# Row maxima on two 64-row tiles of TensorE, one head of a pair in each

## The reference

```
h = layernorm(x) * (1 + ca) + sa
q = h Wq^T; latent = h Wkv_down^T; k = latent Wk_up^T; v = latent Wv_up^T     # 8 heads of 64
attn = softmax(q k^T / 8) ; x = x + ga * (attn v) Wo^T
h = layernorm(x) * (1 + cb) + sb
x = x + gb * (h W^T + pooled(h) disha)
```

## Time and profile before

| | |
|---|---|
| time, median of 3 runs | 3648.74 us (3648.51 to 3649.03) |
| the profiled execution | 3651.17 us, span 3649.2 us |
| granted TensorE clock | 0.983 of full speed |
| TensorE busy | 97% |
| VectorE / ScalarE / GpSimd busy | 67% / 46% / 69% |
| DMA | 9.9% of 16 engines |

### The profile page before, as it was taken

One profiled execution on the slowest core, in us unless ns is written; L12 is line 12 of the kernel. 1 busy time (PEld: TensorE's weight loads), 2 busy tenths in 40 slices (PEclk: granted clock), 3 DMA queues, 4 the chain that ended last, 5 costly groups with the idle time before them and its releaser, 6 DMA issues.

```text
span 3649.2 us, 50991 instructions
## 1 busy us (share of the span) xinstructions
PE 3530.1 (97%) x15014; PEld 1840.0 (50%) x15014; DVE 2446.3 (67%) x2846; ACT 1684.6 (46%) x3075; POOL 2515.4 (69%) x1513
## 2 busy tenths in 40 slices
PE   5999999999999999999999999999999999999997
PEld 3444555545454554545545455454555545555454
DVE  4667667676676767657676576766767667676663
ACT  1445445444454545445454354543545445454443
POOL 1677767676776767668677676866767677686775
PEclk7999999999999999999999999999999999999998
DMA  1101010010101001010010100101010010100101
GB/s 55 35 20 48 24 56 21 30 48 27 47 26 55 18 27 53 24 51 18 33 47 24 51 27 27 50 27 48 21 41 36 27 48 27 53 18 33 35 30 32
DMA packets 98076, 129.24 MB, mean 35 GB/s; under 512 B 11120, under 2 KB 62448, under 8 KB 97776
## 3 DMA queue, kind: packets, MB, share of 16 engines
q1 hardware_dynamic: 97776, 125.64, 9.9%
HBM read 41.11 MB, written 16.81 MB: 16 GB/s over the span
## 4 chain that ended last, share of the span: by engine, by line
PE 94%; DVE 3%; issue 2%; ACT 1%; POOL 0%; DMA 0%; SPq 0%; DVEq 0%; POOLq 0%; ACTq 0%
PE ps_mix L543 28%; PE ps_max L593 18%; PE ps_score L564 14%; PE ps_score L566 13%; PE ps_side_b L531 7%; PE ps_side_b L651 5%; PE ps_side_a L638 4%; PE ps_side_b L669 3%; PE ps_side_a L631 1%; PE ps_side_a L658 1%; DVE h_lo L972 1%; PE ps_side_a L608 0%; DVE recip L931 0%; DVE neg_max L950 0%; PE ps_side_a L622 0%
## 5 line engine op out<-in xcount | busy, mean ns | idle before, releaser
L811 POOL TENSOR_TENSOR prob_sum<-prob_sum,probs 128x1024 f32<-128x1024 f32 x768 | 1837.5, 2393 | 575.7 <-ACT probs L710 518.7
L950 DVE TENSOR_REDUCE neg_max<-ps_max 128x1 f32<-128x1024 f32 x1016 | 1243.5, 1224 | 721.1 <-PE ps_max L593 710.9
L710 ACT ACTIVATE probs<-ps_score 128x512 f32<-128x512 f32 x2048 | 1113.0, 596 | 1140.9 <-PE ps_score L566 1129.2
L543 PE MATMUL ps_mix<-probs,values 128*64 128x512 f32 x4096 | 1109.5, 620 | 0.0
L564 PE MATMUL ps_score<-query,key_hi 128*128 128x512 f32 x2048 | 839.8, 410 | 37.2 <-issue 35.8
L566 PE MATMUL ps_score<-query_m,key_lo 128*128 128x512 f32 x2048 | 810.2, 396 | 0.0
L593 PE MATMUL ps_max<-key_hi,query 128*128 128x512 f32 x2032 | 749.8, 450 | 5.1 <-DVE neg_max L950 5.0
L593 PEld LDWEIGHTS ps_max<-key_hi,query 128*128 128x128 f32 x2032 | 304.5, 189 | 830.4 <-issue 433.6
L811 POOL TENSOR_TENSOR prob_sum<-probs 128x1024 f32<-128x1024 f32 x128 | 305.5, 2387 | 457.7 <-ACT probs L710 457.7
L931 DVE RECIPROCAL recip<-recip 128x128 f32<-128x128 f32 x512 | 481.4, 942 | 17.8 <-ACT recip L761 17.8
L564 PEld LDWEIGHTS ps_score<-query,key_hi 128*128 128x128 f32 x2048 | 387.5, 189 | 155.2 <-issue 73.9
(11 more groups left out here) (115 smaller groups left out, 2701.8 us busy)
## 6 DMA issues: line engine op xcount, KB each, us to landing
query_m<-query SPq DMA_DIRECT2D x128, 512.0 KB, 3.2
x_in<-in_L_attn_x_dram SPq DMA_DIRECT2D x16, 1024.0 KB, 5.5
x_mid<-in_L_attn_x_dram SPq DMA_DIRECT2D x64, 256.0 KB, 6.9
out_dram<-x_mid SPq DMA_DIRECT2D x64, 256.0 KB, 2.2
h_t<-gates_scratch SPq DMA_DIRECT2D x16, 256.0 KB, 6.7
query_m<-max_row SPq DMA_DIRECT2D x128, 4.0 KB
mixed<-in_L_wmod_dram SPq DMA_DIRECT2D x1, 1536.0 KB, 11.3
mixed<-in_L_attn_Wq_dram SPq DMA_DIRECT2D x1, 512.0 KB, 4.9
```

The costliest lines, as they stand in the source:

```text
L543: last = nc.tensor.matmul(ps_mix[g % 2][j * R:j * R + R, :], values[par][:, k, :], probs[:, s % RING, j * HALF:(j + 1) * HALF], start=(k = ...
L710: nc.scalar.activation(probs[:, s % RING, half * HALF:(half + 1) * HALF], ps_score[half], ACT.Exp, scale=SCALE).then_inc(exps_done, 1)
L811: nc.gpsimd.tensor_tensor(out=total[:, :], in0=before, in1=probs[:, s % RING, :], op=ALU.add).then_inc(adds_done, 1)
L950: nc.vector.tensor_reduce(neg_max[:, m:m + 1], z.max_bank(m, ps_max, ps_scores)[:, :], AX_X, ALU.max, negate=True).then_inc(maxima_done, 1)
```

## The change

The row-maximum pass is cut otherwise. Before, a step took 128 queries of one head, high and low parts (128 partitions), by 1024 keys. After, a step takes 128 queries of both heads of a pair, with their high parts alone (64 partitions each), by 512 keys: the even head's matmul reads partitions 0 to 63 and writes the first bank, the odd head's reads 64 to 127 and writes the second. The number of steps, of matmuls and of their columns stays the same. For that odd heads keep their high parts on partitions 64 to 127 and their low parts on 0 to 63 of `query`. The scores' second product pairs `query_m` with `key_lo` and its last row must still be a low-part partition, so the copy to `query_m` swaps the halves of the odd head: three DMAs in place of one, and the waits on `query_m_copied` count 48 instead of 16. VectorE's reduction gives two maxima (one per head) of half the keys, into `neg_half`; at the last step of a group a small operation takes the minimum of the two halves (they are negated) into `neg_max`, behind a wait for the reduction, and a new semaphore, `maxima_joined`, tells TensorE's max_row.

```diff
--- before.py
+++ after.py
@@ -272,6 +272,7 @@
         values = [sb(f"values{i}", [P, NT, R]) for i in range(2)]
         query = sb("query", [P, H, T], F32R)
         query_m = sb("query_m", [P, 2, T], F32R)
+        neg_half = sb("neg_half", [P, 2, STEPS])
         neg_max = sb("neg_max", [P, STEPS])
         max_row = [sb(f"max_row{i}", [NT, P], F32R) for i in range(2)]
         probs = sb("probs", [P, RING, T])
@@ -358,6 +359,7 @@
         exps_done = sem("exps_done")
         max_scores_ready = sem("max_scores_ready")
         maxima_done = sem("maxima_done")
+        maxima_joined = sem("maxima_joined")
         full = [sem("a_full"), sem("b_full")]
         a_full, b_full = full
         a_drained = sem("a_drained")
@@ -455,11 +457,14 @@
                             elif j in (2, 4):
 
                                 need_alone(sp, b_drained, z.before(1))
-                            sp.dma_start(query_m[:, j % 2, :].rearrange("p (h n) -> p h n", h=2).bitcast(F32),
-                                         group_queries(j).bitcast(F32)).then_inc(query_m_copied, 16)
+                            even, odd = (group_queries(j)[:, h, :].bitcast(F32) for h in range(2))
+                            to = query_m[:, j % 2, :].rearrange("p (h n) -> p h n", h=2).bitcast(F32)
+                            sp.dma_start(to[:, 0, :], even).then_inc(query_m_copied, 16)
+                            sp.dma_start(to[0:R, 1, :], odd[R:P]).then_inc(query_m_copied, 16)
+                            sp.dma_start(to[R:P, 1, :], odd[0:R]).then_inc(query_m_copied, 16)
                         if s == row % STEPS and there:
                             need_alone(sp, a_drained, z.through(0, "max_row", j) + 1)
-                            need_alone(sp, query_m_copied, 16 * (GROUPS * b + j + 1))
+                            need_alone(sp, query_m_copied, 48 * (GROUPS * b + j + 1))
 
                             need_alone(sp, max_row_set, 16 * (GROUPS * b + j))
                             sp.dma_start(query_m[P - 1:P, j % 2, :].bitcast(F32),
@@ -580,7 +585,7 @@
                     if item:
                         b, m = item
                         gm, unit = divmod(m, NT)
-                        hm, qt = 2 * (gm // 2) + unit // 4, 4 * (gm % 2) + unit % 4
+                        p, qt, kh = gm // 2, 4 * (gm % 2) + unit // 2, unit % 2
                         kpar = (1 - z.par) if s >= MAX_LAG else z.par
                         if m % (2 * NT) == 0:
 
@@ -589,10 +594,11 @@
                             need(pe, b_drained, z.through(1, *made) + 1 if here else z.before(1))
                         need(pe, maxima_done, STEPS * b + m - (0 if z.has_c else 1))
                         bank = z.max_bank(m, ps_max, ps_scores)
-                        for half in range(2):
-                            last = nc.tensor.matmul(bank[:, half * HALF:(half + 1) * HALF],
-                                                    query[:, hm, qt * P:(qt + 1) * P],
-                                                    key_hi[kpar][:, half * HALF:(half + 1) * HALF],
+                        for j in range(2):
+                            rows = slice(j * R, (j + 1) * R)
+                            last = nc.tensor.matmul(bank[:, j * HALF:(j + 1) * HALF],
+                                                    query[rows, 2 * p + j, qt * P:(qt + 1) * P],
+                                                    key_hi[kpar][rows, kh * HALF:(kh + 1) * HALF],
                                                     start=True, stop=True)
                         last.then_inc(max_scores_ready, 1)
                     for kind, i, bank, b, w in z.at(s):
@@ -626,7 +632,7 @@
                             p, half = divmod(i, 2)
                             last = project(side, slice(p * P, (p + 1) * P), slice(half * HALF, (half + 1) * HALF))
                         elif kind == "max_row":
-                            need(pe, maxima_done, STEPS * b + NT * (i + 1))
+                            need(pe, maxima_joined, GROUPS * b + i + 1)
                             need(pe, a_drained, count)
                             last = nc.tensor.matmul(side[0:NT, 0:P], neg_max[:, NT * i:NT * (i + 1)], ident[:, :],
                                                     start=True, stop=True)
@@ -731,7 +737,7 @@
                             need(act, b_full, count + 1)
                             p, half = divmod(i, 2)
                             for j in range(2):
-                                nc.scalar.activation(query[0:R, 2 * p + j, half * HALF:(half + 1) * HALF],
+                                nc.scalar.activation(query[j * R:(j + 1) * R, 2 * p + j, half * HALF:(half + 1) * HALF],
                                                      ps_b[j * R:(j + 1) * R, :], ACT.Copy).then_inc(query_hi_done, 1)
                         elif kind == "latent":
                             need(act, b_full, count + 1)
@@ -947,7 +953,15 @@
                     if item:
                         b, m = item
                         need(dve, max_scores_ready, STEPS * b + m + 1)
-                        nc.vector.tensor_reduce(neg_max[:, m:m + 1], z.max_bank(m, ps_max, ps_scores)[:, :], AX_X, ALU.max, negate=True).then_inc(maxima_done, 1)
+                        gm, unit = divmod(m, NT)
+                        group = slice(NT * gm, NT * (gm + 1))
+                        nc.vector.tensor_reduce(neg_half[:, unit % 2, group].rearrange("p (h q) -> p q h", h=2)[:, unit // 2, :],
+                                                z.max_bank(m, ps_max, ps_scores)[:, :].rearrange("p (h n) -> p h n", h=2),
+                                                AX_X, ALU.max, negate=True).then_inc(maxima_done, 1)
+                        if unit == NT - 1:
+                            need(dve, maxima_done, STEPS * b + m + 1)
+                            nc.vector.tensor_tensor(neg_max[:, group], neg_half[:, 0, group], neg_half[:, 1, group],
+                                                    ALU.min).then_inc(maxima_joined, 1)
                     divide(z, s)
                     if s == GATE_STEPS[2][z.has_c] and z.has_o:
                         need(dve, w_out_hi_done, z.o + 1)
@@ -989,8 +1003,10 @@
                             p, half = divmod(i, 2)
                             cols = slice(half * HALF, (half + 1) * HALF)
                             for j in range(2):
-                                last = nc.vector.tensor_tensor(query[R:P, 2 * p + j, cols], ps_b[j * R:(j + 1) * R, :],
-                                                               query[0:R, 2 * p + j, cols].bitcast(F32), ALU.subtract)
+                                last = nc.vector.tensor_tensor(query[(1 - j) * R:(2 - j) * R, 2 * p + j, cols],
+                                                               ps_b[j * R:(j + 1) * R, :],
+                                                               query[j * R:(j + 1) * R, 2 * p + j, cols].bitcast(F32),
+                                                               ALU.subtract)
                             last.then_inc(b_drained, 1)
                         elif kind == "latent":
                             need(dve, key_hi_done, 4 * b + 2 * (i + 1))
```

## The result

The changed kernel takes 3690.89 us (median of 4, 3687.66 to 3695.62) against 3648.89 us for the one before: a ratio of 1.0112, 95% interval 1.0095 to 1.013. It is slower by 42 us; the forecast was 18 us slower. The profiled execution spans 3685.8 us at a mean granted clock of 0.976 (before 3649.2 at 0.983).

| what | before | after |
|---|---|---|
| row-maximum pair | L593 | L599 |
| scores | L564, L566 | L569, L571 |
| projections (latent, query) | L531 | L536 |
| ffn | L669 | L675 |
| VectorE's reduction | L950 | L958 |

What follows compares the result with a forecast made beforehand. The prediction took TensorE's own instructions, in their order, to bound the kernel. Its terms, +41 - 32 + 4 + 5 = +18 us, gave 3667 us against the median of the runs, 0.5% slower, with a range of 3552 to 3700.

Steps and rivals of the forecast that it cites:

- +41 - 32 + 4: TensorE's row-maximum pairs: +41 us before scores, out_proj or latent projections, -32 before column tiles, +4 before fp32 transposes.
- a sign of being wrong in kind: TensorE's long waits for L950 or L980 growing beyond tens of us, or waits for the rows of maxima appearing.
- The halves at once: Row-maximum pair on TensorE: both 64-row matmuls run concurrently, streaming 0.232 us instead of 0.464, saving 0.232.
- part 2: Row-maximum pair on TensorE: two different 64x128 weights share one load path, adding 0.106 us per pair.
- rival A: Row-maximum pair on TensorE: the two weight loads go at once; -84 us, 3565 us, chance 0.15.
- part 3: Work behind the row-maximum pair on TensorE finds another array cut: 0.095 us plus the exposed load, except before column tiles.
- part 4: VectorE: reduction unchanged at 1024 elements a row; the join, 128 times 0.28 us, lies five steps ahead of its reader.
- The ffn steps: TensorE's ffn behind a pair: VectorE's chain begins 0.126 us earlier but gains the join (0.10 + 0.182); +5 us.
- part 5: Query copies on SP's queue: three DMAs instead of one cost SP 1.3 us, covered by over 10 us; nothing added.

Runs made afterwards that it cites:

- reduce_join: The changed kernel with the join as a one-input reduction in place of the two-input operation: 3581.52 us, ratio 0.9813 to the kernel before.
- same_half: reduce_join with both matmuls of a pair on the lower 64 rows, old query layout and one DMA: 3772.74 us, ratio 1.0346 to the kernel before.
- before_plus_join: The kernel before with only a two-input join added at the same place on VectorE: 3749.46 us, ratio 1.0274.
- before_reduce_join: The kernel before with a one-input reduction as the join at the same place on VectorE: 3670.13 us, ratio 1.0058.
- late_join: reduce_join with the join moved behind the division and low parts in VectorE's step: 3578.54 us, ratio 0.9814 to the kernel before.
- layout_only: The kernel before with only the new query layout and its three DMAs, old row-maximum pass: 3652.74 us, ratio 1.0007.

## Why the prediction was wrong

The sign came out right, by luck; the size did not (18 us, measured 42). The forecast had TensorE's own instructions cost 13 us more (+41 - 32 + 4) and its waits 5. The instructions cost 108 us less (reduce_join), and the kernel is slower through waits for VectorE alone. Two terms were wrong, each by more than the whole result, with opposite signs. The forecast had named a sign of being wrong in kind, waits for L950 or L980 grown beyond tens of us, and it appeared: the waits for L980 went from 7.7 to 67.1 us, and those for L972 from 11.4 to 46.4.

**The halves at once: right.** The second matmul starts with the first (the pair spans 0.50, one lasts 0.497), and same_half shows the 0.23 that this saves. The Trainium skill, "TensorE: Matmul & The Clock Gate", section "Part 3: Packing small matmuls", has a packed pair last one matmul and a few ns; the row agrees.

**The second weight load (part 2, +0.106 on every pair, 108 us in all): wrong, it costs nothing.** The reading of the earlier trace rows was right for fp32. The step that failed was carrying it to fp32r: the forecast's own rows had a fp32r load at 189 ns where a fp32 load had 140, so the two types load differently, and the share was doubled all the same. Both loads are over in 0.19 us, and the next work starts 0.43 behind the pair, which is what rival A had said (chance 0.15).

**The third change of cut (part 3): right.** 0.095 and the exposed load stand in the timeline (0.106 + 0.232 + 0.095 = 0.433, measured 0.43, and a score matmul of 0.50) and in same_half's 125 us. With the second load struck out, by the rows of after a pair with scores behind it is 0.43 + 0.106 - 0.57 = -0.034 (544, -18 us), with column tiles 0.43 - 0.66 = -0.23 (256, -59 us), with transposes 0.43 + 0.055 - 0.57 = -0.085 (160, -14 us): -91 us. The pairs ahead of the ffns are shorter too, 0.50 instead of 0.73, 60 times: -14 us. Together -105, where reduce_join's busy time has -108.

**The join (0.18 us in the ffn's sum and part 4): wrong, it takes 0.96, and it moves others.** The step that failed took a small operation's price from L867, which reads one tensor. The join reads two from SBUF, and operations of that kind were in the trace of before: L972, 128x512, had a mean of 1318 ns where L998 (`key_lo`, the same size, with one input in PSUM) had 685. The forecast did not tell the two kinds apart. The Trainium skill, "SBUF — State Buffer", section "Who interferes with whom", says that an operation of VectorE with two SBUF inputs contends with GpSimd's reads and one side blocks in full, while a reduction never does; the traces agree: the two-input joins of the changed kernel and of before_plus_join that began while GpSimd ran end 20 to 32 ns behind its operation, and the reductions in reduce_join and before_reduce_join, 240 of them begun while GpSimd ran, took at most 174 ns. A rule that speaks against the change stood there and was not weighed.

**The ffn steps (+5 us) and the latent projections (not priced): wrong.** The ffn starts 1.49 behind its pair, where the forecast's terms give 0.79 + 0.079 = 0.87: against before it is 60 x 0.70 = 42 us. With the one-input join it is 0.84: the sum was right but for the join's price. Of the 112 us of added idle, 56 are ahead of the ffns (the 42, and the 14 by which their pairs are shorter), 35 ahead of the projections and 21 ahead of pairs. Low parts that are not behind the join lengthened too (2.31 us against 1.32, and 58 of 64 held against 45): VectorE's whole order slid against GpSimd's sums. Which slide does what is not settled: in late_join an earlier start of the low parts bought only a longer wait.

**The copies (part 5): right.** Nothing, by layout_only.

The sum as measured: -105 us on TensorE's own instructions (-91 and -14), +119 us of idle time, and up to 26 us of lower clock, which makes 14 to 40 against the 36.6 of the two spans. With the one-input join, rival A's time of 3565 is missed by 16 us: TensorE waits 8.6 us more than before ahead of the projections for the first norm's low parts (which are at 1.57 us) and 7.8 more ahead of pairs, and the forecast had priced neither.

## What to carry to other kernels

A small operation that a change adds is priced by the class of its operands, not by its size: on VectorE, two inputs in SBUF beside a busy GpSimd cost up to 2 us here, whatever the size, and held back all that was queued behind. Look in the trace for operations of the same class, see whether they end with GpSimd's, and use a one-input form or a place where nothing urgent stands behind. Half-height tiles side by side save a stream and cost a change of the array's cut (0.095 us and an exposed load of 0.106), which leaves 0.03 us for a pair with scores behind it; they pay where the neighbours change cut anyway. When a bound engine gets faster, the engines that it now meets at another moment are the next price.

## What was not expected of the hardware

- Two fp32r loads of 64x128 into the two halves take 183 ns each at once, one of 128x128 takes 189; in fp32 they take 186 each, one of 128x128 takes 141.
- An operation of 8 results a row on VectorE took 0.17 to 2.07 us with two inputs in SBUF, and 0.169 to 0.173 as a reduction with one. Each of the 120 that began while GpSimd ran ended 21 to 27 ns behind GpSimd's operation.
- After waits of 0.75 and 1.89 us within some 3 us the granted clock was 0.54 over 3.2 us. Over the execution the time at the lower level grew with the waits: the mean clock was 0.983 before, 0.976 after, and 0.982 with the one-input join.
